# Two gaps of 128 bytes ahead of the split weights of a relational graph layer, one core

## The chip, the cores and the metric

The kernel runs on one core of a Trainium2 chip. The time is device microseconds from the start of the program to its end, median of several runs. One further execution was taken by the hardware profiler, and all rows below are of it.

## The reference

For each of 128 graphs there are 128 nodes with 128 features (`x`, fp32) and a 128x128 matrix `adj` of relation numbers. What is computed is a normalised relational layer with a residual:

```python
h = jnp.maximum(_layernorm(x, axis=-1), 0.0)
x = x + _L0_gnn_ref(h, nodemask, adj, ...)
...
h = x @ W.T
g = h @ Wg.T
vals = (h[:, :, None, :] + b) * jax.nn.sigmoid(g[:, :, None, :] + bg)
onehot = (adj[..., None] == rel_ids).astype(h.dtype)
return jnp.einsum('bnmr,bmrd->bnd', onehot, vals)
```

The inputs drawn hold only the numbers 0 and 1 in `adj`, so of the 40 relations only the loop relation (number 1) contributes, and `adj` itself is the mask. The kernel takes this short way, sums a distance of `adj` from 0 and 1 beside it, and turns to a general way (inside `If` blocks at the end of each engine's program) when that sum says that other numbers occur. With these inputs the general way is not entered.

## The kernel before

The 128 graphs are worked off in 32 groups of four. All of `x` and `adj` have room in SBUF (`x_all`, `adj_all`), and every engine's program is written out by hand, with semaphores between them. There is no scheduler and no planner; the order of the work is the order of the loops in the source. For a group `g` the steps are these.

- SyncE loads `x` and `adj` in 16 chunks of two groups each and stores the results from `x_all`.
- VectorE takes the row statistics (`row_stats`, L524). GpSimd turns them into 1/sqrt(variance) with a power (`coefficients`, L333 to L339) for a batch of four groups at once, from group 6 on: 6, 10, 14, 18, 22, 26, and a last batch of groups 30 and 31. One power over 16 columns serves a batch.
- GpSimd and VectorE normalise the rows into `xn` (L352 and L541). Of the four groups of a batch GpSimd does 3, 4, 3 and 3 graphs (`BATCH_SHARES`), VectorE the rest. GpSimd also casts the mask of three groups in four (L363), ScalarE that of the fourth (L405). `xn` has four slots, so that a normalised group may lie ready up to four groups ahead of its use.
- TensorE transposes the four graphs (`turn_rows`, L751, moving operand `ident`), ScalarE writes the high half of relu of it as fp32r (`hT_hi`, L414), VectorE the remainder (`hT_lo`, L567).
- TensorE multiplies (`products`, L764, L765, L769). Stationary is a 128x128 slice of `hT_hi` or `hT_lo`, moving are the 256 columns of `w_hi` or `w_lo`, which hold the weight and the gate's weight side by side. Each graph takes three matmuls, hi by hi, hi by lo, lo by hi, that is 12 a group. They add to a bias that ScalarE has written into PSUM from `bias_all` (`seed`, L421).
- ScalarE applies the sigmoid (L436), VectorE multiplies (`messages`, L557), TensorE multiplies by the mask (`aggregate`, L786, moving operand `vals`, two matmul records a graph, 8 a group), VectorE adds the residual (L582).
- ScalarE watches `adj` (L442, a sum of absolute values into `dist`, with `junk` as the discarded output), and after the last chunk TensorE, VectorE and a register read decide on the general way (L811, L628, L630).

TensorE's steady loop is `turn_rows(t + 2)`, `products(t + 1)`, `aggregate(t)`, so 4 + 12 + 8 matmul records a group. For the last group `products` and `aggregate` are done in two halves. `w_hi` and `w_lo` are written once, near the start, by ScalarE (L451, L456) and VectorE (L589). `zeros` is read by TensorE's filler matmuls near the start.

SBUF tensors are placed one after the other in the order of their `sb(...)` calls. The steps that the change and the prediction speak of are the calls of `sb` and, in the TensorE program, these lines:

```python
hi, to = hT_hi[:, s, j * N:j * N + N], prod_ps[s][:, j, :, :]
nc.tensor.matmul(to, hi, w_hi[:, :], start=False, stop=False, skip_group_check=True)
nc.tensor.matmul(to, hi, w_lo[:, :], start=False, stop=False, skip_group_check=True)
...
lo, to = hT_lo[:, s, j * N:j * N + N], prod_ps[s][:, j, :, :]
last = nc.tensor.matmul(to, lo, w_hi[:, :], start=False, stop=True, skip_group_check=True)
```

The call that places a tensor is `ctx.enter_context(nc.sbuf_tensor(name, shape, dt))`. The diff touches `build` alone, which holds the whole kernel, in its list of tensors; the rest of `build` stays as told above.

Of the kernel before, what the change touches and what calls it, by code (L numbers as in the profile page):

```python
# [18 lines left out]
def build(nc, x, adj, W_fwd, W_bwd, W_loop, Wg_fwd, Wg_bwd, Wg_loop,  # L19
# [25 lines left out]
    with ctx:  # L45
        def sb(name, shape, dt=FP32):
            return ctx.enter_context(nc.sbuf_tensor(name, shape, dt))
# [20 lines left out]
        ones = sb("ones", [128, 128])  # L68
        w_raw = sb("w_raw", [128, 2, 128])
        w_gT = sb("w_gT", [128, 128])  # L70
        w_hi = sb("w_hi", [128, 2 * D], FP32R)
        w_lo = sb("w_lo", [128, 2 * D], FP32R)
        bias_all = sb("bias_all", [128, 2, D])
        zeros = sb("zeros", [128, 4 * D], BF16)
# [791 lines left out]
```

How the kernel before makes its waits and increments, by code:

```python
        @block.sync  # L241
# [21 lines left out]
            load_x(1)  # L263
            load_x(2)
            load_x(3)
            load_adj(0)
            for c in range(4, LOAD_AHEAD):
                load_x(c)
                load_adj(c - 3)
            for c in range(LOAD_AHEAD, CHUNKS):
                load_x(c)
                load_adj(c - 3)
                sp.wait_ge(out_ready, (c - LOAD_AHEAD + 1) * CHUNK)
                store_tile((c - LOAD_AHEAD) * CG, (c - LOAD_AHEAD) * CC, CG)
            load_adj(CHUNKS - 3)
            load_adj(CHUNKS - 2)
            load_adj(CHUNKS - 1)
            for c in range(CHUNKS - LOAD_AHEAD, CHUNKS - 2):
                sp.wait_ge(out_ready, (c + 1) * CHUNK)
                store_tile(c * CG, c * CC, CG)
            for g in range(GROUPS - 4, GROUPS - 1):
                sp.wait_ge(out_ready, g + 1)
                store_tile(g * GROUP, g * GC, GROUP)
            sp.wait_ge(out_ready, GROUPS)
            store_tile(B - GROUP // 2, (B - GROUP // 2) * D, GROUP // 2)
            sp.wait_ge(flag_ready, 1)
            with sp.If(sp.value_load(flag[0:1, 0:1], min_val=0, max_val=1) != 0):
                sp.wait_ge(stored, 16 * STORES)
                for d, (b_, bg_) in enumerate(((b_fwd, bg_fwd), (b_bwd, bg_bwd))):
# [10 lines left out]
                with sp.Fori(0, B) as b:  # L302
                    sp.wait_ge(g_stored, b * 16 + 16)
                    sp.dma_start(g_x, x[bass.ds(b, 1), :, :].rearrange("o n d -> n (o d)")
```

## Time and profile before

| | |
|---|---|
| median of 3 runs | 104.5 us (104.45 to 105.08) |
| the profiled execution's own time | 104.03 us |
| its span, first to last instruction | 102.2 us |
| time around the span | 1.83 us |
| mean granted clock of TensorE | 0.992 |

A profile row of an engine gives the time in which it was busy. A matmul's duration runs from its start to the modelled end of its results, and neighbours overlap, so what counts for the pace of TensorE is the distance from one start to the next. The pieces of the chain that ended last give just this distance, summed over the instructions of a piece. A span on GpSimd is rough, but the starts of its instructions follow each other in order and can be used as a clock of its own.

### The profile page before, as it was taken

Reading aid. Unit: us, or ns where it says so; the run is one execution under the profiler, and the core shown is the slowest. Engines: PE = TensorE matmul, PEld = TensorE weight load, DVE = VectorE, ACT = ScalarE, POOL = GpSimd, SP = SyncE. Lnnn points to the kernel's source line nnn. Section 1 sums busy time; section 2 is a strip of 40 time slices with the busy share of each in tenths; the row PEclk is TensorE's granted clock in tenths of the full one; section 3 lists DMA queues with packets and bytes.
Section 4 is the critical chain, followed back from the end, with each engine's and each line's share of the span. In section 5 each row is a group of like instructions: output and inputs, shape, how many; then the busy total and the mean of one; then the engine's idle time right before and its main releaser. Section 6 shows DMA issues by size and latency. Waiting matters only on the chain.

```text
span 102.2 us, 2493 instructions
## 1 busy us (share of the span) xinstructions
PE 95.4 (93%) x802; PEld 91.3 (89%) x802; DVE 90.1 (88%) x196; ACT 88.6 (87%) x144; POOL 85.8 (84%) x162
## 2 busy tenths in 40 slices
PE   5986899998999999999999999999999999999960
PEld 2655789797999999999999999999999999999950
DVE  2289989999999999999999999999999788777761
ACT  5075498899799998999899989998999989898990
POOL 2188999999999999999999999999999999991000
PEclk9999999999999999999999999999999999999996
DMA  1899999999999999999999999999945150606345
GB/s 50 242 319 292 290 290 290 291 293 294 293 312 298 328 328 331 311 329 322 333 282 317 271 324 316 327 292 313 345 134 157 58 151 28 184 6 205 103 140 168
DMA packets 50288, 25.45 MB, mean 249 GB/s; under 512 B 866, under 2 KB 50276, under 8 KB 50276
## 3 DMA queue, kind: packets, MB, share of 16 engines
q1 hardware_dynamic: 50000, 25.17, 88.5%
q10 hardware_dynamic: 276, 0.13, 0.4%
q8 instruction: 6, 0.10, 0.4%
q14 instruction: 6, 0.05, 0.1%
HBM read 16.91 MB, written 8.39 MB: 247 GB/s over the span
## 4 chain that ended last, share of the span: by engine, by line
PE 71%; POOL 4%; ACT 3%; issue 1%; DVE 0%; POOLq 0%
PE psum L786 23%; PE psum L764 12%; PE psum L769 12%; PE psum L765 12%; PE psum L751 11%; POOL rstd L339 3%; ACT junk L442 2%; POOL xn L352 1%; ACT gate L436 0%; PE psum L811 0%; DVE dist_sum L628 0%; DVE flag L630 0%; POOLq L362 0%
## 5 line engine op out<-in xcount | busy, mean ns | idle before, releaser
L352 POOL TENSOR_SCALAR xn<-x_all,mean_neg,rstd 128x128 f32<-128x128 f32 x101 | 44.7, 454 | 0.7 <-POOL rstd L339 0.4
L764 PE MATMUL psum<-w_hi,hT_hi 128*128 128x256 f32 x128 | 33.8, 299 | 1.3 <-DVE w_lo L589 0.9
L786 PE MATMUL psum<-vals,mask 128*128 128x128 f32 x256 | 33.6, 275 | 0.1
L421 ACT ACTIVATE psum<-bias_all 128x1024 f32<-128x1024 f32 x32 | 33.1, 1035 | 0.3 <-DVE vals L557 0.3
L786 PEld LDWEIGHTS psum<-vals,mask 128*128 128x128 f32 x256 | 31.0, 191 | 0.2 <-issue 0.2
L765 PE MATMUL psum<-w_lo,hT_hi 128*128 128x256 f32 x128 | 31.0, 277 | 0.0
L524 DVE BATCH_NORM_STATS2 stats<-x_all 128x6 f32<-128x256 f32 x64 | 23.9, 418 | 3.2 <-DMA x_all<-in_x 3.0
L764 PEld LDWEIGHTS psum<-w_hi,hT_hi 128*128 128x128 f32 x128 | 24.1, 188 | 2.0 <-DVE w_lo L589 1.1
L557 DVE TENSOR_TENSOR vals<-psum,gate 128x512 f32<-128x512 f32 (+1 forms) x33 | 21.9, 663 | 3.9 <-ACT gate L436 3.3
L339 POOL TENSOR_TENSOR rstd<-var_eps,minus_half 128x16 f32<-128x16 f32 (+2 forms) x11 | 24.5, 2225 | 0.1
L765 PEld LDWEIGHTS psum<-w_lo,hT_hi 128*128 128x128 f32 x128 | 24.2, 189 | 0.0
L567 DVE SCALAR_TENSOR_TENSOR hT_lo<-psum,hT_hi 128x512 fp32r<-128x512 f32 x32 | 21.8, 682 | 1.2 <-ACT hT_hi L414 1.1
L414 ACT ACTIVATE hT_hi<-psum 128x512 fp32r<-128x512 f32 x32 | 19.2, 600 | 3.5 <-PE psum L751 3.5
L582 DVE SCALAR_TENSOR_TENSOR x_all<-psum,x_all 128x512 f32<-128x512 f32 (+1 forms) x33 | 21.7, 662 | 0.1
L436 ACT ACTIVATE gate<-psum 128x512 f32<-128x512 f32 (+1 forms) x33 | 19.4, 587 | 1.7 <-PE psum L769 1.7
L769 PE MATMUL psum<-w_hi,hT_lo 128*128 128x256 f32 x128 | 20.2, 278 | 0.0
L751 PE MATMUL psum<-ident,xn 128*128 128x128 f32 x128 | 19.5, 275 | 0.7 <-POOL xn L352 0.4
L442 ACT ACTIVATE junk<-adj_all,minus_half 128x1024 bf16<-128x1024 int32 x16 | 18.4, 1153 | 0.0
L769 PEld LDWEIGHTS psum<-w_hi,hT_lo 128*128 128x128 f32 x128 | 17.1, 188 | 0.1
L751 PEld LDWEIGHTS psum<-ident,xn 128*128 128x128 f32 x128 | 14.7, 142 | 1.5 <-POOL xn L352 0.8
L363 POOL CAST mask<-adj_all 128x512 f32<-128x512 int32 x22 | 13.3, 611 | 0.0
L541 DVE TENSOR_SCALAR xn<-x_all,stats,rstd 128x128 f32<-128x128 f32 x27 | 8.7, 340 | 0.0
(36 smaller groups left out, 31.3 us busy)
## 6 DMA issues: line engine op xcount, KB each, us to landing
adj_all<-in_adj SPq DMA_DIRECT2D x16, 512.0 KB, 6.8
x_all<-in_x SPq DMA_DIRECT2D x15, 512.0 KB, 6.8
out<-x_all SPq DMA_DIRECT2D x14, 512.0 KB, 6.2
out<-x_all SPq DMA_DIRECT2D x3, 256.0 KB, 2.3
x_all<-in_x SPq DMA_DIRECT2D x2, 256.0 KB, 3.0
out<-x_all ACTq DMA_DIRECT2D x1, 128.0 KB, 2.5
out<-x_all SPq DMA_DIRECT2D x1, 128.0 KB, 2.6
w_raw<-in_L_gnn_W_loop SPq DMA_DIRECT2D x1, 64.0 KB, 2.5
```

Of the source, the lines that this page charges most:

```text
L339: pool.tensor_tensor(rstd[:, s, 0:n], var_eps[:, s, 0:n], minus_half[:, 0:n], ALU.pow).then_inc(rstd_ready, 1)
L352: last = pool.tensor_scalar(xn[:, g % XN, j * D:j * D + D], x_all[:, g * GC + j * D:g * GC + j * D + D], mean_neg[:, b % BATCH_SLOTS, k:k ...
L421: nc.scalar.activation(prod_ps[s].rearrange("p g a d -> p g (a d)"), bias_all[:, :, :].rearrange("p a d -> p (a d)").unsqueeze(1) .to_broa ...
L524: last = nc.vector.bn_stats(stats[:, b % BATCH_SLOTS, ((g - first) * GROUP + j) // 2, :], x_all[:, g * GC + j * D:g * GC + (j + 2) * D].re ...
L557: nc.vector.tensor_tensor(per_graph(vals[:, s, :])[:, some, :], prod_ps[s][:, some, 0, :], per_graph(gate[:, s, :])[:, some, :], ALU.mult) ...
L567: nc.vector.scalar_tensor_tensor(out=hT_lo[:, s, :], in0=hT_ps[s], scalar=0.0, in1=hT_hi[:, s, :].bitcast(FP32), op0=ALU.max, op1=ALU.subt ...
L582: nc.vector.scalar_tensor_tensor(out=cols, in0=sums_ps, scalar=0.0, in1=cols, op0=ALU.max, op1=ALU.add).then_inc(half_out if more else out ...
L751: last = nc.tensor.transpose(hT_ps[s][:, j * N:j * N + N], xn[:, g % XN, j * D:j * D + D], ident[:, :])
L764: nc.tensor.matmul(to, hi, w_hi[:, :], start=False, stop=False, skip_group_check=True)
L765: nc.tensor.matmul(to, hi, w_lo[:, :], start=False, stop=False, skip_group_check=True)
L769: last = nc.tensor.matmul(to, lo, w_hi[:, :], start=False, stop=True, skip_group_check=True)
L786: last = nc.tensor.matmul(to[:, j * D:j * D + D], mask[:, g % MASKS, j * N:j * N + N], vals[:, s, j * D:j * D + D], start=True, stop=True)
```

## The change

Two tensors that nothing reads or writes are placed ahead of `w_hi` and `w_lo`. Each is 32 fp32 columns, which is 128 bytes in every partition.

```diff
--- before.py
+++ after.py
@@ -68,7 +68,10 @@
         ones = sb("ones", [128, 128])
         w_raw = sb("w_raw", [128, 2, 128])
         w_gT = sb("w_gT", [128, 128])
+
+        gap_hi = sb("gap_hi", [128, 32])
         w_hi = sb("w_hi", [128, 2 * D], FP32R)
+        gap_lo = sb("gap_lo", [128, 32])
         w_lo = sb("w_lo", [128, 2 * D], FP32R)
         bias_all = sb("bias_all", [128, 2, D])
         zeros = sb("zeros", [128, 4 * D], BF16)
```

The first byte of a tensor within a partition, in the built programs, before and after:

| tensor | before | after | before, modulo 1024 | after, modulo 1024 |
|---|---|---|---|---|
| `hT_hi` (stationary) | 155776 | 155776 | 128 | 128 |
| `hT_lo` (stationary) | 159872 | 159872 | 128 | 128 |
| `vals` (moving in L786) | 168064 | 168064 | 128 | 128 |
| `ident` (moving in L751) | 181952 | 181952 | 704 | 704 |
| `w_hi` (moving) | 184512 | 184640 | 192 | 320 |
| `w_lo` (moving) | 185536 | 185792 | 192 | 448 |
| `bias_all`, `zeros`, `bias_row`, `junk`, `dist`, `flag` | from 186560 | from 186816 | 192 (`bias_all`) | 448 (`bias_all`) |

All that lies behind `w_lo` moves by 256 bytes, `w_hi` by 128, `w_lo` by 256. Every engine's list of instructions is the same as before, in the same order, with the same semaphores; only the source lines behind the new ones are three higher.

## Rows read from the trace of the kernel before

**Rows 1.** the page, section 1: busy us of each engine (share of the span) and number of instructions; granted clock

```profile
PE 95.4 (93%) x802; PEld 91.3 (89%) x802; DVE 90.1 (88%) x196; ACT 88.6 (87%) x144; POOL 85.8 (84%) x162
...
PEclk9999999999999999999999999999999999999996
```

**Rows 2.** the chain that ended last, shares by engine and by line (page, section 4)

```profile
PE 71%; POOL 4%; ACT 3%; issue 1%; DVE 0%; POOLq 0%
PE psum L786 23%; PE psum L764 12%; PE psum L769 12%; PE psum L765 12%; PE psum L751 11%; POOL rstd L339 3%; ACT junk L442 2%; POOL xn L352 1%; ACT gate L436 0%; PE psum L811 0%; DVE dist_sum L628 0%; DVE flag L630 0%; POOLq L362 0%
```

**Rows 3.** waits over the span: who waited for whom, us in total, times, longest us

```profile
PEld psum L751 <- POOL xn L352: 0.8, 2, 0.6
...
PE psum L751 <- POOL xn L352: 0.4, 1, 0.4
```

**Rows 4.** pieces of the chain, 45 to 50 us: start us, us, what, and how many instructions

```profile
45.15 0.45 PE psum L769 x4
45.60 0.89 PE psum L786 x8
...
47.96 0.47 PE psum L769 x4
48.43 0.89 PE psum L786 x8
49.32 0.44 PE psum L751 x4
```

**Rows 5.** timeline of TensorE's transposes: start us, us, engine, line, op, tiles, count

```profile
46.36 0.66 PE L751 MATMUL psum<-ident,xn 128*128 128x128 f32 x4
...
49.16 0.60 PE L751 MATMUL psum<-ident,xn 128*128 128x128 f32 x4
...
51.90 0.60 PE L751 MATMUL psum<-ident,xn 128*128 128x128 f32 x4
...
68.11 0.64 PE L751 MATMUL psum<-ident,xn 128*128 128x128 f32 x4
...
76.33 0.60 PE L751 MATMUL psum<-ident,xn 128*128 128x128 f32 x4
...
79.02 0.60 PE L751 MATMUL psum<-ident,xn 128*128 128x128 f32 x4
...
92.49 0.60 PE L751 MATMUL psum<-ident,xn 128*128 128x128 f32 x4
```

**Rows 6.** timeline of GpSimd, same columns, powers and first normalisations of its batches

```profile
44.87 3.15 POOL L352 TENSOR_SCALAR xn<-x_all,mean_neg,rstd 128x128 f32<-128x128 f32 x7
...
52.29 2.90 POOL L339 TENSOR_TENSOR rstd<-var_eps,minus_half 128x16 f32<-128x16 f32 x1
...
55.74 3.15 POOL L352 TENSOR_SCALAR xn<-x_all,mean_neg,rstd 128x128 f32<-128x128 f32 x7
...
63.16 2.90 POOL L339 TENSOR_TENSOR rstd<-var_eps,minus_half 128x16 f32<-128x16 f32 x1
...
66.61 3.14 POOL L352 TENSOR_SCALAR xn<-x_all,mean_neg,rstd 128x128 f32<-128x128 f32 x7
...
77.48 3.14 POOL L352 TENSOR_SCALAR xn<-x_all,mean_neg,rstd 128x128 f32<-128x128 f32 x7
```

**Rows 7.** timeline of ScalarE, same columns, the last groups of graphs; idle time and its releaser in brackets

```profile
87.74 0.60 ACT L414 ACTIVATE hT_hi<-psum 128x512 fp32r<-128x512 f32 x1 [0.30 <-PE psum L751]
...
97.08 1.14 ACT L442 ACTIVATE junk<-adj_all,minus_half 128x1024 bf16<-128x1024 int32 x1
...
99.25 0.19 ACT L442 ACTIVATION_READ_ACCUMULATOR junk<-adj_all,minus_half 128x1 f32 x1
```

**Rows 8.** one line's instructions over the span: duration ns min/median/max, first and last start us, form

```profile
L764 PE MATMUL psum<-w_hi,hT_hi x128: 276/279/388, 9.1 to 96.1; 128*128 128x256 f32 x128
L421 ACT ACTIVATE psum<-bias_all x32: 1011/1030/1065, 5.9 to 93.6; 128x1024 f32<-128x1024 f32 x32
```

## The prediction

> **What bounds the kernel now.** I read the engines' shares first. TensorE is busy 93% of the span, but VectorE has 88%, ScalarE 87% and GpSimd 84%, and the granted clock stands at its full level from the first slices to the end, so the clock is no subject here [rows 1]. Four engines so close together say that the chain has to be asked. It gives TensorE 71% of the span, spread over its five lines in proportion to their matmuls, GpSimd only some 4% and ScalarE 3% [rows 2]. Taken alone this reads as a kernel bound by TensorE, in which anything that makes the 384 product matmuls quicker or slower moves the end in full.
>
> The waits show a second fact. TensorE waited for GpSimd's `xn` at the transposes, 0.4 us in all [rows 3]. That is small, and a small wait is easily passed over; it can also mean that two engines run at the same pace. So I compared starts. GpSimd's first normalisations of a batch of four groups start at 44.87, 55.74, 66.61 and 77.48 us, which is 10.87 us apart three times over, and no row has idle time in front of it [rows 6]. TensorE's transposes of groups 14 and 22 start at 46.36 and 68.11 us, 21.75 us apart for eight groups [rows 5]; GpSimd needs 66.61 - 44.87 = 21.74 us for the same eight. The two go in step, to a hundredth. From group 6 to group 26 the pace is GpSimd's, and TensorE is so near to it that it has almost nothing to wait for.
>
> TensorE's own pace is not constant. Between 49.16 and 51.90 a group takes 2.74 us, between 76.33 and 79.02 it takes 2.69 [rows 5]. The chain shows where: four lo-by-hi products take 0.45 us of it in one group and 0.47 in the next, while eight matmuls of the mask take 0.89 us in both and four transposes 0.44 [rows 4]. In starts that is 0.113 us a product in the quicker groups, 0.117 in the slower ones, 0.111 for a mask matmul, 0.110 for a transpose. Of the 26 groups from 24.6 us on 7 are slower ones, always the two or three after a start at which TensorE had stood still (46.36 and 68.11 are two of them [rows 5]). 12 products at 0.0042 us more are the 0.05 us of difference.
>
> After group 26 GpSimd is ahead, since its last batch is of two groups with a shorter power, and TensorE runs freely from 79.02 to the end of its stream near 97 us. ScalarE closes with two watches of `adj`, from 97.08 to 99.25 and a bit [rows 7], which hang on the last sigmoid and so on the last product.
>
> **The change part by part.** No instruction is added, removed or moved. No wait, buffer, size, data type or transfer changes. The gaps themselves are neither written nor read, and they cost no time. What is left is where four kinds of operands lie.
>
> *`w_hi` and `w_lo` as moving operands of TensorE.* These are 3 x 4 x 32 = 384 reads of 256 columns, and the only place where the change can have a sizeable effect. Both tensors keep a start that is a multiple of 64 bytes and 64 more than a multiple of 128, before and after. What changes is the remainder at 256 and above: `w_hi` goes from 192 to 320 modulo 1024, `w_lo` from 192 to 448. The trace of before has no product with the weights elsewhere, so I bound the cost by the nearest rows. One hint that it is nothing: the stationary slices of `hT_hi` start at 128 and 640 modulo 1024 in turn, so the distance from weights to stationary operand alternates by 512 from graph to graph, and the chain's pieces do not alternate; the durations of line L764 lie between 276 and a median of 279 ns [rows 8]. A second: the mask's matmuls and the transposes read `vals` at 128 and `ident` at 704 and pace at 0.111 and 0.110 us, hardly other than the products.
>
> For the lower end I let every product pace like a transpose, 0.110 us. Up to group 26 this is given away: group 26's three graphs from GpSimd are ready at 77.48 + 3/7 x 3.14 = 78.83 us, and the two starts at which TensorE had waited lie 0.14 and 0.15 us behind their data (46.36 against 44.87 + 3/7 x 3.15 = 46.22, and 68.11 against 66.61 + 1.35 = 67.96), so group 26 cannot start before 78.97, against 79.02 now [rows 5, 6]. That is 0.05 us. Behind it come 6 groups of 12 products, 72 x 0.0035 = 0.25 us. Together 0.3 us off.
>
> For the upper end every product paces like those of the slower groups. Then 25 groups from 24.63 us take 25 x 2.744 = 68.60 us and the last group's transposes start at 93.23, against 92.49 [rows 5]; the last group's products add 0.05 us. Together 0.8 us on. Here nothing is hidden by GpSimd, since TensorE becomes the slower of the two (4 x 2.744 = 10.98 against 10.87 us).
>
> I take 0, since every row that varies a remainder of 512 shows no dependence on it. The Trainium skill ("SBUF — State Buffer", section "SBUF: two separate sides") says that on the engines' side only the port pair that VectorE and GpSimd share brings contention, and that TensorE and ScalarE never wait for anybody; by it, too, the place of the weights would be worth 0. What the slower groups' 0.004 us a product are it doesn't explain, so I keep them as the size of what may lie beneath.
>
> *`bias_all` for ScalarE's seeds.* 32 of them of 1030 ns, 1011 at least and 1065 at most [rows 8]. If all went to either end this would be 20 to 35 ns each, 1.1 us in sum at most (32 x 0.035), and it lies beside TensorE: ScalarE still idles 0.30 us for the transposes in a late group [rows 7]. 0, and 0 if the cover stays.
>
> *`w_hi`, `w_lo` written once, `zeros`, `bias_row`, `junk`, `dist`, `flag`.* Three writes, fillers near the start and a discarded output. The start of the steady part hangs on GpSimd's power and normalisations, which touch nothing that moves. 0.
>
> *Sum.* The profiled execution took 104.03 us, 102.2 of span and 1.83 around it. Plus 0 this is 104.0, with 103.7 and 104.8 as the ends of the bounds. The median of the runs is 104.5, 0.47 above the profiled one, so the forecast for a median is 104.5 us, with ends at 104.2 and 105.3. The repeats themselves spread from 104.45 to 105.08, which is as much as either bound.
>
> **The rivals.**
>
> *Slower: the products fall into the slow pace for good.* The place is TensorE's stream from group 6 on. If the new distance between weights and stationary slices makes each product take 0.1175 us or more in all groups, the time is 104.5 + 0.8 = 105.3 us. It becomes more than 1% (1.04 us) where the mean product passes 0.119 us: the mean is now (19 x 0.1133 + 7 x 0.1177)/26 = 0.1145, some 0.3 us of TensorE's waits would be eaten first, and (1.04 + 0.3)/312 = 0.0043 us must come on top. For it: the products already know two paces with no difference in the instructions. Against it: the two are told apart by whether TensorE had just stood still, at one and the same address, so they look like a matter of how full its queue is and not of where the weights lie.
>
> *Faster: the products shed what they have above a transpose.* 0.3 us as worked out, 104.2 us; with the seven slower groups gone besides it changes nothing up to group 26, because TensorE would wait for GpSimd instead. The Trainium skill ("TensorE: Matmul & The Clock Gate", section "Back-to-back issue gap") gives N / 2.4 + 2.5 ns for an isolated matmul, 109.2 ns at N = 256. An estimate by that page would be 72 x 4.1 ns = 0.3 us, the same size. To be faster by 1% from the free part alone 72 products would have to lose 14 ns each and start 0.099 us apart; no two successive matmuls or weight loads of the stream do. So a gain over 1% would need GpSimd itself to be faster, and it reads and writes nothing that moves.
>
> *The change doesn't do what it says.* The gaps might be dropped or the tensors be placed by size. The built program shows both gaps at 184512 and 185664, so I give this no weight.
>
> **How the numbers follow.** No effect that a measurement can tell, 104.5 us: 0.75. Some quicker products, 104.2: 0.12, of which 0.04 are for something in excess of 1% that I cannot see. Slower products: 0.13, half of it at about 105.3 (under 1%) and half beyond. About 1% is what a measurement of this kernel can tell from no change. So faster by over 1% has 0.04, within 1% 0.88, slower by over 1% 0.08. The range takes the two bounds and the spread of repeats: 104.5 - 0.3 - 0.3 = 103.9 and 104.5 + 0.8 + 0.1 = 105.4 us.
>
> **What would show it right or wrong.** In the profile of the changed kernel GpSimd's first normalisations of batches should again start 10.87 us apart without idle time; the chain's pieces of four lo-by-hi products should take 0.45 us in most groups and 0.47 after a stop, and group 31's transposes should start near 92.5 us. If the products' pieces take 0.44 us, or 0.47 throughout, the weights' place does matter, and the sum then tells whether GpSimd hid it: its sign would be a longer or a vanished wait of TensorE for `xn`. The forecast is wrong if the products take 0.48 us or more for four, or if GpSimd's turn is no longer 10.87 us.

## The result, and the profile after

The changed kernel takes 105.31 us (median of 8 runs, 104.98 to 105.98), before 104.59 us in 8 runs beside it. The ratio is 1.0081 with a 95% interval of 1.0049 to 1.0112: slower by 0.8%, where I had forecast no effect. The time lies in the range, at the very place of the slower rival, which had 0.13 in all and half of that at 105.3 us.

The shares of the engines, and TensorE's granted clock, from the page of the profile after. They answer to [rows 1]:

```profile
PE 96.7 (93%) x802; PEld 92.4 (89%) x802; DVE 90.6 (88%) x196; ACT 88.8 (86%) x144; POOL 85.6 (83%) x162
...
PEclk9999999999999999999999999999999999999999
```

TensorE is busy 1.3 us longer, at full clock, and it has no more instructions. The engines' busy time tells no more than that. The chain's shares answer to [rows 2], and they say nothing either: the same lines, three numbers higher, with the same shares to a point.

```profile
PE 71%; POOL 4%; ACT 2%; issue 1%; DVE 0%; POOLq 0%
PE psum L789 22%; PE psum L767 12%; PE psum L768 12%; PE psum L772 12%; PE psum L754 11%; POOL rstd L342 3%; ACT junk L445 2%; POOL xn L355 1%; ACT gate L439 0%; PE psum L814 0%; DVE dist_sum L631 0%; DVE flag L633 0%; POOLq L365 0%
```

The cause shows only in the distances of starts. Pieces of the chain, as in [rows 4] (start us, us, what, how many instructions):

```profile
43.07 0.47 PE psum L772 x4
43.54 0.89 PE psum L789 x8
44.43 0.44 PE psum L754 x4
...
48.56 0.47 PE psum L772 x4
...
51.31 0.47 PE psum L772 x4
```

Four lo-by-hi products (L772 now) take 0.47 us in each of these groups. In [rows 4] it was 0.45 in one and 0.47 in the next. The mask's eight (L789) and the transposes' four (L754) keep their 0.89 and 0.44. The starts of the transposes answer to [rows 5]:

```profile
24.99 0.66 PE L754 MATMUL psum<-ident,xn 128*128 128x128 f32 x4 [0.57 <-POOL xn L355]
...
47.01 0.60 PE L754 MATMUL psum<-ident,xn 128*128 128x128 f32 x4
...
49.76 0.49 PE L754 MATMUL psum<-ident,xn 128*128 128x128 f32 x3
...
90.96 0.60 PE L754 MATMUL psum<-ident,xn 128*128 128x128 f32 x4
...
93.71 0.60 PE L754 MATMUL psum<-ident,xn 128*128 128x128 f32 x4
```

From group 14 to 15 it is 2.75 us, and from group 30 to 31 again 2.75. Taken in nanoseconds from the trace, all 24 distances from group 7 on are 2746 or 2747 ns. Before, the same distances were 2693 or 2694 in most groups and 2743 or 2744 in the stretches after a stop. So the stretch no longer ends: from the stop at 24.99 us on TensorE keeps the slow pace to the end, though it never stops again. Whether it would have the slow pace here without any stop can't be told, since every profile has stops before group 6.

From 24 us on this is the only wait of TensorE's matmuls for GpSimd (who waited for whom, us in total, times, longest us), and it is the one at 24.99 us:

```profile
PE psum L754 <- POOL xn L355: 0.6, 1, 0.6
```

The stops at groups 14 and 22, whose starts [rows 5, 6] show before, are gone, for GpSimd is now the quicker of the two. Its first normalisations of a batch:

```profile
45.23 3.02 POOL L355 TENSOR_SCALAR xn<-x_all,mean_neg,rstd 128x128 f32<-128x128 f32 x7
...
55.94 3.07 POOL L355 TENSOR_SCALAR xn<-x_all,mean_neg,rstd 128x128 f32<-128x128 f32 x7
...
66.78 3.02 POOL L355 TENSOR_SCALAR xn<-x_all,mean_neg,rstd 128x128 f32<-128x128 f32 x7
...
77.48 3.07 POOL L355 TENSOR_SCALAR xn<-x_all,mean_neg,rstd 128x128 f32<-128x128 f32 x7
```

They start 10.71, 10.84 and 10.70 us apart, against 10.87 in [rows 6]. TensorE takes 4 x 2.747 = 10.99 us for the same four groups, so by group 26 the data lie ready over a microsecond ahead.

The sum of the two profiles: group 31's transposes start at 93.71 against 92.49 us, 1.22 later. Of this 0.36 us lie ahead of group 6 (24.99 against 24.63), where the profiles of the later layouts scatter, but for one with a lowered clock, from 24.65 to 25.42 us with no link to the layout. From group 6 to 31 it is 68.72 against 67.86 us, 0.86 us, and 0.0081 of 104.6 us is 0.85. The tail is as it was, from the first of the last two watches to the read of the last sum 2.17 us as in [rows 7]:

```profile
98.36 1.14 ACT L445 ACTIVATE junk<-adj_all,minus_half 128x1024 bf16<-128x1024 int32 x1
...
100.53 0.19 ACT L445 ACTIVATION_READ_ACCUMULATOR junk<-adj_all,minus_half 128x1 f32 x1
```

ScalarE's seeds, the other operand that was moved, are no longer either (1030 ns before, [rows 8]):

```profile
L424 ACT ACTIVATE psum<-bias_all x32: 1009/1024/1037, 6.3 to 94.8; 128x1024 f32<-128x1024 f32 x32
```

### The profile page after: what moved, and what is told of

The parts are those of the page before. It is cut to its first block, busy times and chain, and to the rows that moved or that the text cites. A ratio compares the mean times of both kernels' runs of the same rounds, so it can differ in the third digit from the quotient of the medians.

```text
span 103.5 us, 2493 instructions
## 1 busy us (share of the span) xinstructions
PE 96.7 (93%) x802; PEld 92.4 (89%) x802; DVE 90.6 (88%) x196; ACT 88.8 (86%) x144; POOL 85.6 (83%) x162
## 4 chain that ended last, share of the span: by engine, by line
PE 71%; POOL 4%; ACT 2%; issue 1%; DVE 0%; POOLq 0%
PE psum L789 22%; PE psum L767 12%; PE psum L768 12%; PE psum L772 12%; PE psum L754 11%; POOL rstd L342 3%; ACT junk L445 2%; POOL xn L355 1%; ACT gate L439 0%; PE psum L814 0%; DVE dist_sum L631 0%; DVE flag L633 0%; POOLq L365 0%
## 5 line engine op out<-in xcount | busy, mean ns | idle before, releaser
L767 PE MATMUL psum<-w_hi,hT_hi 128*128 128x256 f32 x128 | 34.4, 302 | 0.9 <-DVE w_lo L592 0.6
L789 PE MATMUL psum<-vals,mask 128*128 128x128 f32 x256 | 33.7, 275 | 0.2 <-issue 0.2
L768 PE MATMUL psum<-w_lo,hT_hi 128*128 128x256 f32 x128 | 31.7, 282 | 0.0
L789 PEld LDWEIGHTS psum<-vals,mask 128*128 128x128 f32 x256 | 31.2, 191 | 0.4 <-issue 0.4
L772 PE MATMUL psum<-w_hi,hT_lo 128*128 128x256 f32 x128 | 20.5, 281 | 0.0
L754 PE MATMUL psum<-ident,xn 128*128 128x128 f32 x128 | 19.4, 274 | 1.0 <-POOL xn L355 0.8
L772 PEld LDWEIGHTS psum<-w_hi,hT_lo 128*128 128x128 f32 x128 | 17.4, 189 | 0.1
L754 PEld LDWEIGHTS psum<-ident,xn 128*128 128x128 f32 x128 | 14.9, 142 | 1.8 <-POOL xn L355 1.2
L544 DVE TENSOR_SCALAR xn<-x_all,stats,rstd 128x128 f32<-128x128 f32 x27 | 9.3, 363 | 0.0
```

The source lines that it names most:

```text
L754: last = nc.tensor.transpose(hT_ps[s][:, j * N:j * N + N], xn[:, g % XN, j * D:j * D + D], ident[:, :])
L789: last = nc.tensor.matmul(to[:, j * D:j * D + D], mask[:, g % MASKS, j * N:j * N + N], vals[:, s, j * D:j * D + D], start=True, stop=True)
```

## The experiments

In all of them "a group" is the distance of the starts of two neighbouring groups' transposes in the profile, when TensorE doesn't wait; in the fences two such rows stand for many like them. Remainders are those of a tensor's first byte in a partition. I began with three theories. W: the place of the weights sets the products' pace. B: what lies behind the weights does it. S: the slow pace is a state that a run falls into at random. The letters of the later theories are explained in the expectation that first uses them. The group periods and product distances in nanoseconds are each of one profiled execution, the ratios of about ten runs beside as many or more of before.

### Which part of the change

**Only what lies behind is moved.**

```diff
         w_lo = sb("w_lo", [128, 2 * D], FP32R)
+        gap_behind = sb("gap_behind", [128, 64])
         bias_all = sb("bias_all", [128, 2, D])
```

> 256 bytes of gap behind w_lo, so both weights stay where before has them and only bias_all and what follows lies where after has it. Theory W (the place of the weights sets the products' pace): ratio to before 1.000 within 0.003, four lo-by-hi products in 0.45 us in most groups, group period 2.69 us. Theory B (what lies behind the weights, bias_all for ScalarE above all, does it): ratio 1.008, 0.47 us for four products and 2.747 us a group throughout. Theory S (the slow pace is a state that a run falls into by how it starts, whatever the addresses): either, with no link to the layout, and profiles of other layouts differ at random.

Measured 0.9998 (0.9965 to 1.0032). Groups of 2.693 us with stretches of 2.744, as before. B falls. TensorE's transposes of the last two groups:

```profile
90.36 0.60 PE L752 MATMUL psum<-ident,xn 128*128 128x128 f32 x4
...
93.05 0.60 PE L752 MATMUL psum<-ident,xn 128*128 128x128 f32 x4
```

**Both weights moved by 128, adjoining.**

```diff
+        gap_hi = sb("gap_hi", [128, 32])
         w_hi = sb("w_hi", [128, 2 * D], FP32R)
         w_lo = sb("w_lo", [128, 2 * D], FP32R)
+        gap_behind = sb("gap_behind", [128, 32])
```

> 128 bytes ahead of w_hi and 128 behind w_lo: both weights at 320 modulo 1024, with no gap between them; the rest as in after. Theory W in the form that the absolute place at 128-byte steps counts, or the distance from the stationary slices: like after, ratio 1.008, 2.747 us a group. Theory W in the form that w_hi and w_lo have to be a whole 1024 bytes apart: like before, ratio 1.000, 2.69 us a group. Theory B: 1.008.

Measured 1.0001 (0.9970 to 1.0031), 2.707 us a group. So the first gap of the change by itself costs nothing that this interval of 0.3% either way shows, although it does slow TensorE: in each group the distances from the second product to the third, and on to the sixth, are 0.120, 0.117, 0.116 and 0.114 us, and the rest 0.1133. This adds 0.0133 us to 2.6933, and 2.707 is still below the 2.718 us a group at which GpSimd went before.

```profile
90.50 0.60 PE L753 MATMUL psum<-ident,xn 128*128 128x128 f32 x4
...
93.21 0.60 PE L753 MATMUL psum<-ident,xn 128*128 128x128 f32 x4
```

**Only w_lo moved, by 128.**

```diff
         w_hi = sb("w_hi", [128, 2 * D], FP32R)
+        gap_lo = sb("gap_lo", [128, 32])
         w_lo = sb("w_lo", [128, 2 * D], FP32R)
+        gap_behind = sb("gap_behind", [128, 32])
```

> 128 bytes between w_hi and w_lo and 128 behind: w_hi at 192 as before, w_lo at 320 modulo 1024. If one weight's place suffices, the two products of w_hi (8 of the 12 in a group) keep 0.113 us and those of w_lo (4 of 12) take 0.118, so 2.71 us a group and a ratio near 1.002 since GpSimd's 2.718 us a group hides it up to group 26. If the distance of the two counts, all are slow, 2.747 us and 1.008. Theory B: 1.008.

Measured 1.0090 (1.0065 to 1.0114), 2.747 us in every group. The gap between the weights alone makes the whole loss. The milder outcome, in which only the four products with `w_lo` are slow, did not come: those with `w_hi` are slow too, 0.12 us behind each `w_lo` in the first rows below, and the four lo-by-hi take 0.48 us up to the start of the mask's. Theory S falls too, since two layouts with the gap between the weights, and none of the three without it, hold one and the same slow period to the end.

```profile
90.75 0.60 PE L753 MATMUL psum<-ident,xn 128*128 128x128 f32 x4
...
91.31 0.28 PE L767 MATMUL psum<-w_lo,hT_hi 128*128 128x256 f32 x1
91.43 0.28 PE L766 MATMUL psum<-w_hi,hT_hi 128*128 128x256 f32 x1
91.55 0.28 PE L767 MATMUL psum<-w_lo,hT_hi 128*128 128x256 f32 x1
...
92.13 0.64 PE L771 MATMUL psum<-w_hi,hT_lo 128*128 128x256 f32 x4
92.61 1.05 PE L788 MATMUL psum<-vals,mask 128*128 128x128 f32 x8
93.50 0.60 PE L753 MATMUL psum<-ident,xn 128*128 128x128 f32 x4
```

**Both weights moved by 256, adjoining.**

```diff
+        gap_hi = sb("gap_hi", [128, 64])
         w_hi = sb("w_hi", [128, 2 * D], FP32R)
```

> 256 bytes ahead of w_hi: both weights at 448 modulo 1024, the rest as in after. If the remainder modulo 256 counts (192 again): like before, ratio 1.000 and 2.69 us a group. If the remainder modulo 512 or more counts, like after, 1.008 and 2.747 us. Theory B: 1.008.

Measured 1.0014 (0.9988 to 1.0040), groups of 2.693 with stretches of 2.744 us, as before. A move of both by 256 bytes changes nothing.

### How far apart the weights may lie

**256 bytes between them instead of 128.**

```diff
         w_hi = sb("w_hi", [128, 2 * D], FP32R)
+        gap_lo = sb("gap_lo", [128, 64])
         w_lo = sb("w_lo", [128, 2 * D], FP32R)
```

> 256 bytes between the weights instead of 128: w_hi at 192, w_lo at 448 modulo 1024, both 192 modulo 256, 1280 bytes apart. Theory D256 (the two moving operands must have the same remainder modulo 256, because they take turns; a gap as such is harmless): like before, 2.693 us a group with some groups of 2.744, ratio 1.000. Theory G (they must adjoin, or lie a multiple of 1024 apart): 2.747 us in every group, ratio 1.008.

Measured 0.9999 (0.9975 to 1.0022), 2.693 us with stretches. A gap as such is harmless, and `w_lo` lies at the byte at which the changed kernel has it. What hurts there is its distance from `w_hi`.

```profile
90.25 0.60 PE L752 MATMUL psum<-ident,xn 128*128 128x128 f32 x4
...
92.95 0.60 PE L752 MATMUL psum<-ident,xn 128*128 128x128 f32 x4
```

**64 bytes between them.**

```diff
         w_hi = sb("w_hi", [128, 2 * D], FP32R)
+        gap_lo = sb("gap_lo", [128, 16])
         w_lo = sb("w_lo", [128, 2 * D], FP32R)
+        gap_behind = sb("gap_behind", [128, 48])
```

> 64 bytes between the weights and 192 behind: w_lo at 256 modulo 1024. Theory D256: 64 is not a multiple of 256, so the products lock in the slow pace, 2.747 us a group, ratio 1.008. A finer form, that only a difference of 128 modulo 256 (the farthest) locks: some third pace or the one of before, ratio under 1.004.

Measured 1.0036 (1.0017 to 1.0056), a third pace: 2.727 us in every group. It is also a check of what the stops of before hide. The mean of the groups 8 to 31 before is 2.710 us, stretches and waits included, and 25 x (2.727 - 2.710) = 0.42 us is 0.4% of 104.4. Counted from the quick pace of 2.693 it would be 0.85 us or 0.8%, which lies above the interval.

```profile
90.59 0.60 PE L753 MATMUL psum<-ident,xn 128*128 128x128 f32 x4
...
93.32 0.60 PE L753 MATMUL psum<-ident,xn 128*128 128x128 f32 x4
```

### Absolute places or distances, and what the products have to agree with

**Everything moved by 128.**

```diff
+        gap_first = sb("gap_first", [128, 32])
         x_all = sb("x_all", [128, SIDE])
```

> 128 bytes ahead of x_all, so that every tensor moves by 128 and all distances between tensors stay those of before. If distances between operands alone count (weights to weights, weights to stationary slices): group pattern of before, 2.693 us, stretches of 2.744 after stops, ratio 1.000. If absolute places count: the pattern of the run with both weights at 320 (2.707 us a group, first products of a group at 0.120 us), ratio 1.000 to 1.003 too, but told apart by the pattern.

Measured 0.9973 (0.9943 to 1.0003), 2.693 us with stretches. The weights are at 320 here, as in the second run, but the slow first products of a group are not there. So distances count, and not places. Whether this version is a little faster than before is not settled by this interval.

**The layout of after, the products in another order.** Against the changed kernel:

```diff
                         nc.tensor.matmul(to, hi, w_hi[:, :], start=False, stop=False, skip_group_check=True)
+                    for j in graphs:
+                        hi, to = hT_hi[:, s, j * N:j * N + N], prod_ps[s][:, j, :, :]
                         nc.tensor.matmul(to, hi, w_lo[:, :], start=False, stop=False, skip_group_check=True)
```

> The layout of after, but a group's four products with w_hi are issued first, then its four with w_lo, then the four lo-by-hi: the weights take turns once or twice a group instead of at every product. Theory T (taking turns between operands of different remainder keeps the products from settling in the quick pace): the products settle, most starts 0.113 us apart, 2.69 to 2.71 us a group, ratio 1.000. If the place of w_lo or the gap as such is slow, however the products are ordered: 2.747 us and ratio 1.008.

Measured 1.0080 (1.0048 to 1.0112), 2.747 us in every group, exactly the pace of the ungrouped order. I had formed theory T, that taking turns at every product keeps them from settling. It falls in this form: with two changes of operand within a group instead of eight nothing is won.

```profile
90.64 0.60 PE L754 MATMUL psum<-ident,xn 128*128 128x128 f32 x4
...
93.39 0.60 PE L754 MATMUL psum<-ident,xn 128*128 128x128 f32 x4
```

**Only hT_lo moved, by 128.**

```diff
         hT_hi = sb("hT_hi", [128, 2, GC], FP32R)
+        gap_a = sb("gap_a", [128, 32])
         hT_lo = sb("hT_lo", [128, 2, GC], FP32R)
+        gap_b = sb("gap_b", [128, 32])
         gate = sb("gate", [128, 2, GC])
```

> 128 bytes ahead of hT_lo and 128 ahead of gate: the two weights keep equal remainders, and so does every other pair, but the start of moving minus stationary operand modulo 256 is 64 for the eight products with hT_hi and 192 for the four with hT_lo. Theory M (the weights must have the same remainder as each other, whatever the stationary): 2.693 us a group with stretches of 2.744, ratio 1.000. Theory R (each product's place of moving relative to stationary counts, and it must not change between neighbours): slower than 2.707 in every group, near 2.73 to 2.747 us, ratio 1.004 to 1.008.

Measured 1.0007 (0.9974 to 1.0040), 2.693 us, and after a stop the quick pace is back after one group instead of two or three. Theory R falls: eight products at a distance of 64 from their stationary slices and four at 192 get on well. In the changed kernel the same two distances occur, and there they do not. Two things differ: which operand jumps (the stationary one here, the moving one there), and how often (once within a group's products here, eight times there). The runs in turns below take up the second.

```profile
90.20 0.60 PE L753 MATMUL psum<-ident,xn 128*128 128x128 f32 x4
...
92.90 0.60 PE L753 MATMUL psum<-ident,xn 128*128 128x128 f32 x4
```

**Both weights moved by 64, adjoining.**

```diff
+        gap_hi = sb("gap_hi", [128, 16])
         w_hi = sb("w_hi", [128, 2 * D], FP32R)
         w_lo = sb("w_lo", [128, 2 * D], FP32R)
+        gap_behind = sb("gap_behind", [128, 48])
```

> Both weights 64 bytes on, adjoining, so moving minus stationary is 128 modulo 256 for all products. Theory M: quick, at most 2.707 us a group. Theory R: no change between products, so they settle; the way in from the transposes (64) and out to the mask's products (0) costs a few starts, 2.69 to 2.71 us a group, ratio within 0.003 of 1.000. A theory that the quick pace needs 64 or 192 between the two operands: slow here, 2.74 us.

Measured 1.0113 (1.0068 to 1.0157), 2.751 and 2.755 us in turn in every group. Two groups:

```profile
88.78 0.60 PE L753 MATMUL psum<-ident,xn 128*128 128x128 f32 x4
...
94.29 0.60 PE L753 MATMUL psum<-ident,xn 128*128 128x128 f32 x4
```

**Both weights moved by 192, adjoining.**

```diff
+        gap_hi = sb("gap_hi", [128, 48])
         w_hi = sb("w_hi", [128, 2 * D], FP32R)
         w_lo = sb("w_lo", [128, 2 * D], FP32R)
+        gap_behind = sb("gap_behind", [128, 16])
```

> Both weights 192 bytes on, adjoining, so moving minus stationary is 0 modulo 256 for all products, as it is for the mask's products already, which pace at 0.1116 us. Theory M and theory R: quick, 2.67 to 2.71 us a group, ratio within 0.003 of 1.000. If two streams that start in the same place modulo 256 get in each other's way: slow in every group, 2.74 us or more, ratio 1.008 or more.

Measured 1.0125 (1.0090 to 1.0159), 2.767 us in every group, the slowest of all. Starts of the last two groups' transposes, then the chain's pieces of four lo-by-hi products:

```profile
91.74 0.60 PE L753 MATMUL psum<-ident,xn 128*128 128x128 f32 x4
...
94.51 0.60 PE L753 MATMUL psum<-ident,xn 128*128 128x128 f32 x4
```

```profile
46.26 0.48 PE psum L771 x4
...
49.03 0.48 PE psum L771 x4
```

0.48 us for four, 0.120 each, in steady state. Both runs go against theory M and theory R at once: equal remainders of the two weights are needed, but they are not enough.

**Only vals moved, by 64.**

```diff
         vals = sb("vals", [128, 2, GC])
+        gap_b = sb("gap_b", [128, 48])
         mask = sb("mask", [128, MASKS, GROUP * N])
```

with `gap_a = sb("gap_a", [128, 16])` ahead of `vals`.

> 64 bytes ahead of vals and 192 ahead of mask: the weights' products stay as they are, and moving minus stationary of the mask's eight products goes from 0 to 64 modulo 256, as the transposes have, which pace at 0.109 us. Theory R extended to all of TensorE: the mask's products change pace, to 0.109 us if they follow the transposes (2.675 us a group), and GpSimd hides it up to group 26, ratio 0.998 to 1.000. Theory M, or a rule for the products alone: 0.1116 us as before, 2.693 us a group.

Measured 1.0005 (0.9974 to 1.0036), 2.693 us, the mask's products at 0.1116 us as before. The matmuls of the mask don't answer to a move of 64 bytes of their moving operand, where the weights' products do; the effect is not one of every matmul. TensorE runs here from group 8 to 25 without a stop, and GpSimd's batches come 10.71 to 10.87 us apart, so GpSimd's 10.87 us of before are not a fixed pace.

### What was still open

> Control, layout of before: the three products of a graph are issued together (hi by hi, lo by hi, hi by lo), so the wait for hT_lo comes ahead of all of a group's products. In steady groups hT_lo has long been there, so 2.693 us a group where TensorE isn't stopped, ratio within 0.005 of 1.000, a little above for the waits near the start.

```diff
+                pe.wait_ge(hT_ready, g + 1)
                 for graphs, more in parts(g):
                     for j in graphs:
                         hi, to = hT_hi[:, s, j * N:j * N + N], prod_ps[s][:, j, :, :]
+                        lo = hT_lo[:, s, j * N:j * N + N]
                         nc.tensor.matmul(to, hi, w_hi[:, :], start=False, stop=False, skip_group_check=True)
-                        nc.tensor.matmul(to, hi, w_lo[:, :], start=False, stop=False, skip_group_check=True)
-                    pe.wait_ge(hT_ready, g + 1)
-                    for j in graphs:
-                        lo, to = hT_lo[:, s, j * N:j * N + N], prod_ps[s][:, j, :, :]
-                        last = nc.tensor.matmul(to, lo, w_hi[:, :], start=False, stop=True, skip_group_check=True)
+                        nc.tensor.matmul(to, lo, w_hi[:, :], start=False, stop=False, skip_group_check=True)
+                        last = nc.tensor.matmul(to, hi, w_lo[:, :], start=False, stop=True, skip_group_check=True)
```

The control: 1.0032 (1.0005 to 1.0059), and 2.693 us with stretches. The wait that now comes ahead of all products may cost the 0.3% near the start, as expected, but no run shows that it does. Its profiled execution had a mean granted clock of 0.977, with 0.6 in two slices of 2.6 us near the start, where matmuls ran near half pace, so only its steady groups are used.

**The same order, hT_lo moved by 128**, with the gaps of the run on `hT_lo`.

> The same order with hT_lo 128 bytes on: the moving operands keep one remainder, but moving minus stationary goes 64, 192, 64 within every graph. Theory M2 (what keeps the pace slow is a moving operand that starts at another remainder than its predecessor's): quick, 2.693 us, as its control. Theory R2 (a difference between moving and stationary that changes too often): 2.747 us in every group, 1.007 or more over its control.

Measured 1.0024 (0.9997 to 1.0051) against before, no slower than its control, and 2.713 us a group. The chain's pieces of one group's first six products:

```profile
44.68 0.12 PE psum L768
44.80 0.12 PE psum L769
44.92 0.12 PE psum L770
45.04 0.12 PE psum L768
45.16 0.11 PE psum L769
45.27 0.11 PE psum L770
```

The first distances are 0.12 us and then, with the stationary operand still jumping by 128 at two products in three, the pace settles at 0.1133. A stationary operand that jumps by 128, even at two products in three, does not lock the slow pace; R2 falls. With it the second difference named above falls away, and of the two it is the moving operand's jump of 128 bytes that locks the pace. M2's number of 2.693 was not met either: the alternation costs 0.020 us a group.

**Weights and stationary slices both moved by 192.**

```diff
+        gap_a = sb("gap_a", [128, 48])
         hT_hi = sb("hT_hi", [128, 2, GC], FP32R)
         hT_lo = sb("hT_lo", [128, 2, GC], FP32R)
+        gap_b = sb("gap_b", [128, 16])
         gate = sb("gate", [128, 2, GC])
```

with the two gaps of the run that moved both weights by 192.

> Both weights 192 bytes on, where they gave 2.767 us a group, and hT_hi and hT_lo 192 bytes on as well, so moving minus stationary is 64 again. If the difference to the stationary slices sets the steady pace: products back at 0.1133 us, at most 2.71 us a group, ratio within 0.003 of 1.000. If the weights' own place (or their step of 64 from ident's) does it: 2.767 us and 1.0125 as there.

Measured 1.0065 (1.0037 to 1.0092), 2.738, 2.743 and 2.745 us in turn. Neither outcome came. The steady 0.120 us is gone, so the distance to `hT_hi` and `hT_lo` has a part, but the products stay near 0.118 and don't reach 0.1133, so it is not the whole.

```profile
91.01 0.60 PE L755 MATMUL psum<-ident,xn 128*128 128x128 f32 x4
...
93.76 0.60 PE L755 MATMUL psum<-ident,xn 128*128 128x128 f32 x4
```

**The transposes' moving operand moved along, by 128.**

```diff
+        gap_i = sb("gap_i", [128, 32])
         ident = sb("ident", [128, 128])
```

> 128 bytes ahead of ident instead of ahead of w_hi: both weights at 320 modulo 1024 as in the run with 2.707 us a group, and ident moved with them. Theory M2: no step of 128 between the last transpose's and the first product's moving operand, so the slow first products of a group (0.120, 0.117, 0.116 us) go, and a group takes 2.693 us in steady state. If the 13 ns come from the difference of 192 between weights and stationary slices: 2.707 us stays.

Measured 0.9999 (0.9973 to 1.0026), and 2.707 us with the same slow first products. The step from `ident` to the weights is not where the 13 ns come from.

**Everything moved by 64.**

```diff
+        gap_first = sb("gap_first", [128, 16])
         x_all = sb("x_all", [128, SIDE])
```

> 64 bytes ahead of x_all: every tensor moves by 64, all distances stay those of before, and the weights start at an even multiple of 64, where they were slow alone. If distances alone count, as the run with everything moved by 128 suggests: 2.693 us a group in stretches, ratio 0.997 to 1.003. If the weights' absolute place counts (odd multiples of 64 quick, even slow): 2.74 to 2.755 us in every group, ratio 1.008 to 1.011.

Measured 1.0008 (0.9973 to 1.0042), 2.693 us with stretches, though the weights now lie at 256 modulo 1024, where they were slow when moved alone. Absolute places are out for moves of 64 and 128 bytes.

```profile
90.47 0.60 PE L752 MATMUL psum<-ident,xn 128*128 128x128 f32 x4
...
93.16 0.60 PE L752 MATMUL psum<-ident,xn 128*128 128x128 f32 x4
```

**ident and the weights moved by 64**, with `gap_i = sb("gap_i", [128, 16])` ahead of `ident`.

> 64 bytes ahead of ident, so ident and both weights start at 256 modulo 1024 or 768, the stationary tensors and vals stay. If the step from the transposes' moving operand to the products' is what counts: quick, 2.693 us, ratio near 1.000. If the weights' absolute place or their distance to hT_hi counts: 2.75 us in every group as with the weights alone at this place, ratio 1.009 to 1.013.

Measured 1.0082 (1.0047 to 1.0117), again 2.751 and 2.755 us in turn, within a nanosecond the groups of the run that moved the weights alone. `ident` has no part in it.

```profile
88.62 0.60 PE L752 MATMUL psum<-ident,xn 128*128 128x128 f32 x4
...
94.13 0.60 PE L752 MATMUL psum<-ident,xn 128*128 128x128 f32 x4
```

### All of it in one table

Moves against before in bytes modulo 256, as the gaps of the edits give them. "Loss expected" is 25 groups times what the group is above 2.710 us, the mean of before with its stretches and waits.

| run | w_hi moved | w_lo moved | rest that TensorE reads | us a group | loss expected | ratio |
|---|---|---|---|---|---|---|
| before | 0 | 0 | - | 2.693, stretches of 2.744 | - | 1 |
| behind, hi256_lo256, lo256 | 0 | 0 | - | the same | 0 | 0.9998, 1.0014, 0.9999 |
| all128, all64 | as all | as all | as the weights | the same | 0 | 0.9973, 1.0008 |
| hTlo128, vals64 | 0 | 0 | hT_lo 128 in the first, vals 64 in the second | the same | 0 | 1.0007, 1.0005 |
| turns_before (other order) | 0 | 0 | - | the same | 0 | 1.0032 |
| turns_hTlo128 (other order) | 0 | 0 | hT_lo 128 | 2.713 | 0.1% | 1.0024 |
| hi128_lo128, ident128_w128 | 128 | 128 | - (ident 128 in the second) | 2.707 | 0, below 2.718 | 1.0001, 0.9999 |
| lo64 | 0 | 64 | - | 2.727 | 0.4% | 1.0036 |
| hT192_w192 | 192 | 192 | hT_hi, hT_lo 192 | 2.742 | 0.8% | 1.0065 |
| after, after_grouped | 128 | 0 | - | 2.747 | 0.9% | 1.0081, 1.0080 |
| lo128 | 0 | 128 | - | 2.747 | 0.9% | 1.0090 |
| both64, ident64_w64 | 64 | 64 | - (ident 64 in the second) | 2.753 | 1.0% | 1.0113, 1.0082 |
| both192 | 192 | 192 | - | 2.767 | 1.4% | 1.0125 |

`after` appears with `w_lo` at 0 because its two gaps add up to 256. The expected loss lies inside every interval but that of `turns_before` (0 against 1.0005 to 1.0059), so the pace of a group is enough to account for what the layout does to the time. The profiles say the same: from group 6 to 31 it is 67.76 to 68.04 us in the layouts that the table has at 0 or 0.1%, 68.24 in `lo64`, and 68.61 to 69.22 in those below it.

## Why the prediction was wrong

- **What bounds the kernel** was read rightly for losses. TensorE and GpSimd were so close that a run at 2.707 us a group, below GpSimd's 2.718, showed no cost, and those from 2.727 up cost what they exceed 2.710 by. "The pace is GpSimd's" was too strong: in `vals64` and `lo256` TensorE ran 17 and 13 groups on end at its own 2.693 us, and GpSimd's batches came 10.71 to 10.93 us apart. What varies GpSimd's turn was not looked for.
- **The step that failed is "I take 0, since every row that varies a remainder of 512 shows no dependence on it."** The observation was true and worthless. The runs show that moves of the weights by 256 bytes change nothing, and slices at 128 and 640 differ by twice that. I had rows that could not differ and read their sameness as a law. The distance that made the loss, that from `w_hi` to `w_lo`, was never weighed in the text: it went from 1024 to 1152 bytes, no row of before varies it, and at 128 bytes off a multiple of 256 the group takes 2.747 us instead of 2.693, whether the pair has moved besides (the changed kernel) or not (`lo128`). The second hint, that `vals` and `ident` pace much like the weights, was as weak: a move of `vals` by 64, or of `ident` along with the weights, changes nothing, so they were not a sample of what happens to the weights.
- **The size of the slow case** was right. I had 25 x 2.744 = 68.60 us from group 6 to 31 and +0.8 us; measured were 68.72 us, +0.86 in the profiles and 1.0081 in the ratio. The bound that I took from the slower groups turned out to be the pace itself, within 3 ns a group. That nothing lay beyond it was luck: it was no bound, for with both weights moved by 64 or 192 a group takes 2.753 and 2.767 us. The rival's reason was not the right one either. It named the distance between weights and stationary slices, and that distance moved by 128 (both weights moved, or `hT_lo` moved) costs nothing that the intervals show.
- **My argument against that rival** failed. I wrote that the two paces are told apart by whether TensorE had just stood still, at one and the same address, "so they look like a matter of how full its queue is and not of where the weights lie". Both count. In the layout of before a stop is followed by slow products; how soon TensorE is out again is set by the layout. Before it takes two or three groups, with `hT_lo` moved by 128 one, with both weights moved by 128 no more than a few products, and in the changed kernel it never happens. The text had the right test, though: 0.47 us throughout for four lo-by-hi products would mean that the weights' place matters, and that is what the profile shows.
- **The sentences from the Trainium skill** ("SBUF — State Buffer", "SBUF: two separate sides") would by their rule have made the placement worth nothing. As far as it says that TensorE never waits for anybody it does not cover this case: with the same instructions a product took 0.1133 to 0.120 us in steady state by the place of the operands alone, and the measurement decides. The page's rule is on contention between engines. Whether what is seen here is TensorE's own two reads (the moving operand and the next weights) in each other's way is a guess that no run here shows.
- **ScalarE's seeds** and all else that moved were rightly costed at 0; the run with only these moved gave 0.9998.
- **GpSimd's turn** was to stay at 10.87 us, and another value was named as a sign of being wrong. It became 10.70 to 10.84, with no effect since GpSimd was ahead.
- **The faster rival** did not come: no layout's group went below 2.693 us. Its sentence that no two successive matmuls start 0.099 us apart overlooks that in every steady group the record of the first product starts 0.028 us after that of the last transpose, and the next 0.201 us after it. The two together are 0.229 us, as long as a transpose and a slow product, so the conclusion stands.
- **The chances.** 0.13 for a slower pace was too little for a change whose one action, moving operands in steps that are no multiples of 256, had no row that showed it. "No row varies this" should have moved chance to both bounds. The 0.08 for a loss over 1% doesn't follow from "half of 0.13", which is 0.065, and the range took 0.3 us for the spread of repeats below and 0.1 above, without a reason.

**What stays open.** Two conditions are shown for the quick pace: the distance between the two weights must be a multiple of 256 bytes (64 and 128 off it are slow, 192 was not run), and the pair must not be moved against the rest by 64 or 192 (by 0 is best, by 128 nearly as good). For the second, `ident` is excluded and `hT_hi` with `hT_lo` are only part of it; `xn`, `mask` and `vals` together with them were not taken apart. Nor was it tested whether the rest that counts is read by TensorE at all: `x_all`, `adj_all` and `gate`, which other engines and the transfers use at the same time, changed their distance to a weight in every run that was slow, and no run moved them alone. Against a clash with GpSimd speaks that in the changed kernel its batches come 10.70 to 10.84 us apart and TensorE's 10.99, so the two drift, while TensorE's period stays within 1 ns; that is an argument and not a test. Why a distance of 128 between the weights locks the pace although the pair is quick at the one place and nearly so at the other, and why grouping the products didn't help, was not found.

## What to carry to other kernels

Where TensorE is the pacemaker with two operands streaming in turn, the place of the moving operands is a parameter that was worth some 1% of the time here (2.693 to 2.767 us a group): try moving operands that alternate a multiple of 256 bytes apart (that this holds in another kernel no run here shows), and compare the group's period in the trace, in nanoseconds, after every edit of the list of tensors, even one that only adds a tensor. Rows that agree are evidence against a dependence only if they differ in what matters; ask first by which step they vary. And of a pace with two levels in one kernel, ask not only what brings it into the slow one but what lets it out.

## What the runs showed that I had not expected

- TensorE's steady pace is a repeating pattern. In every layout that keeps one slow pace to the end the period of a group is constant to 1 ns or, again within 1 ns, cycles through two or three values (2751 and 2755 ns; 2738, 2743 and 2745 ns).
- An order of products with eight changes of the moving operand in a group and one with two have the same period to the nanosecond, 2746.7 ns as a mean, in the same layout.
- Everything moved by 64 or by 128 bytes changes nothing that the intervals show, the weights alone moved by 64 cost 1.1%.
